# Row maxima computed one query block ahead of their scores, with a head's integer keys kept on chip

## The reference

```python
q = (x @ Wq + bq).reshape(1, B * N, H, hd)          # 1600 queries, H = 16 heads of hd = 16
kv = (cond @ Wkv + bkv).reshape(1, -1, 2, H, hd)    # 23104 keys
q = _fq_sym(q * scale, axis=-1)                     # 8 bit per row: step * integer
k = _fq_sym(k, axis=-1)
v = _fq_sym(v, axis=2)
attn = softmax(einsum('bhqd,bhkd->bhqk', q, k))
attn = _fq_unsigned(attn, axis=-1)                  # round(attn / (row maximum / 255))
out = einsum('bhqk,bhkd->bhqd', attn, v)
```

## Time and profile before

| | us |
|---|---|
| median of 3 runs | 8869.47 (8868.29 to 8872.59) |
| the profiled execution | 8867.96 |
| its span in the trace | 8866.1 |
| PE busy | 8189.6 (92%) |
| DVE busy | 6542.9 (74%) |
| ACT busy | 5480.9 (62%) |
| POOL busy | 5204.2 (59%) |

### The profile page before, as it was taken

One profiled execution on the slowest core, in us unless ns is written; L12 is line 12 of the kernel. 1 busy time (PEld: TensorE's weight loads), 2 busy tenths in 40 slices (PEclk: granted clock), 3 DMA queues, 4 the chain that ended last, 5 costly groups with the idle time before them and its releaser, 6 DMA issues.

```text
span 8866.1 us, 223739 instructions
## 1 busy us (share of the span) xinstructions
PE 8189.6 (92%) x60312; PEld 2600.3 (29%) x60312; DVE 6542.9 (74%) x6161; ACT 5480.9 (62%) x12138; POOL 5204.2 (59%) x3573
## 2 busy tenths in 40 slices
PE   8954999999999999999999999999999999988688
PEld 4510222222222222222222222222222222222343
DVE  8989777777777777777777777777777777720466
ACT  2300776767676767676767676767767676767333
POOL 5733665656565656565656565656656565666356
PEclk9955999999999999999999999999999999999789
DMA  5663011110102020202020202010111101020000
GB/s 162 209 163 93 12 26 20 21 24 18 27 13 33 11 34 12 34 12 34 12 34 12 34 11 34 12 28 17 25 20 24 21 18 28 17 42 7 10 4 4
DMA packets 305414, 303.94 MB, mean 34 GB/s; under 512 B 50718, under 2 KB 297802, under 8 KB 300458
## 3 DMA queue, kind: packets, MB, share of 16 engines
q1 hardware_dynamic: 304682, 303.13, 15.7%
q10 hardware_dynamic: 672, 0.16, 0.0%
HBM read 226.31 MB, written 76.71 MB: 34 GB/s over the span
## 4 chain that ended last, share of the span: by engine, by line
PE 63%; DVE 17%; issue 13%; POOL 2%; DVEq 1%; ACT 1%; DMA 1%; SPq 0%; ACTq 0%; POOLq 0%
PE psum L1395 21%; PE psum L1364 18%; DVE mpart L1185 14%; PE psum L1322 13%; PE psum L1374 4%; PE psum L1287 2%; POOL mix L391 1%; ACT y L1084 1%; PE psum L653 1%; DVEq L1185 1%; PE psum L1356 1%; DVE act_c L532 1%; PE psum L1420 1%; POOL kq L933 1%; POOL kq L926 1%
## 5 line engine op out<-in xcount | busy, mean ns | idle before, releaser
L1185 DVE TENSOR_REDUCE mpart<-psum 128x978 f32 x4992 | 5654.8, 1172 | 1510.3 <-PE psum L1322 1399.1
L1084 ACT ACTIVATE y<-psum 128x400 f32<-128x400 f32 x11520 | 5082.2, 504 | 2078.9 <-PE psum L1395 2011.6
L1004 POOL TENSOR_SCALAR xh<-y 128x1600 f16<-128x1600 f32 x2880 | 4397.9, 1527 | 2830.7 <-PE psum L1374 2025.1
L1395 PE MATMUL psum<-QT,K 99*128 x11520 | 3104.3, 340 | 61.0 <-ACT y L1084 54.7
L1364 PE MATMUL psum<-y,ones 128*17 128x400 f32 x23048 | 2539.2, 507 | 0.0
L1322 PE MATMUL psum<-K,QS 48*128 48x489 bf16 x9984 | 1782.8, 390 | 322.6 <-DVE mpart L1185 207.6
L1395 PEld LDWEIGHTS psum<-QT,K 99*128 x11520 | 879.3, 97 | 2495.0 <-issue 2294.7
L1374 PE MATMUL psum<-xh,vwin 128*16 128x400 f16 x11528 | 1019.6, 335 | 0.7 <-POOL xh L1004 0.7
L1322 PEld LDWEIGHTS psum<-K,QS 48*128 48x128 bf16 x9984 | 464.7, 93 | 1680.1 <-issue 873.5
L1364 PEld LDWEIGHTS psum<-y,ones 128*17 128x17 f32 x23048 | 402.4, 95 | 618.2 <-issue 617.8
L1374 PEld LDWEIGHTS psum<-xh,vwin 128*16 128x16 f16 x11528 | 322.6, 90 | 628.6 <-POOL xh L1004 364.5
(11 more groups left out here) (180 smaller groups left out, 2138.6 us busy)
## 6 DMA issues: line engine op xcount, KB each, us to landing
K<-kT_parts SPq DMA_DIRECT2D x204, 240.0 KB, 8.3
vwin<-v_int SPq DMA_DIRECT2D x579, 80.0 KB, 1.9
K<-kT_parts SPq DMA_DIRECT2D x772, 45.8 KB
kT_parts<-part SPq DMA_DIRECT2D x135, 256.0 KB, 3.2
K<-kT_parts SPq DMA_DIRECT2D x102, 242.0 KB, 8.4
src<-in_ctx_dram SPq DMA_DIRECT2D x46, 512.0 KB, 4.6
v_float<-kv SPq DMA_DIRECT2D x45, 512.0 KB, 5.2
vin<-v_float SPq DMA_DIRECT2D x9, 2560.0 KB, 10.1
```

What stands on the lines that cost most here:

```text
L1004: pool.tensor_scalar(xh[:, g % YR, :, :], y[:, g % YR, :, :], INT_STEP, 0.0, ALU.mult, ALU.add)\
L1084: act.activation(y[:, s % YR, j, :], s2_bank(GT * s + j), ACT.Exp).then_inc(exp_done, 1)
L1185: dve.tensor_reduce(mpart[:, t, ds(2 * cp + j, 1)], s1_buf(n)[:, :, 0:CHALF], AX.XY, ALU.max)\
L1395: pe.matmul(s2_bank(t), K3[0:MROW, h % 2, ds(c * REGION + t * P, P)], queries, start=True, stop=True).then_inc(s2_ready, 1)
```

## The change

Jobs of the maxima pass run one **block** ahead of their scores instead of one head. A block's 400 queries are three tiles of 128 (`PT` = 3) and 16 rows that are left; the 4 x 16 rows left of a head share one extra tile. A block's 3 bodies hold 3 x 24 jobs of the next block and 6 of the extra tile of the next head: 26 in a body, as before. Nine of the 72 ("lead") are for the block after the next, done after the turn of maxima. The prologue has 96 jobs and 9 lead jobs in place of 312. All 16 heads now hold jobs; those of the last block are for a head that does not exist and are not used.

`maxima` now comes once a block, inside body c = 2: DVE before the jobs of group 10, the transpose in group 12 between tiles 1 and jobs, ACT's copy between exp 1 and exp 2 of group 12, and three DMAs on SP (six at a head's end) in place of one on ACT. The first job after it uses the PSUM buffer that ACT's copy frees.

All 24 chunks of integer keys of a head stay in `K1`; they are exchanged for the next head's in block 2 of each head, in three bursts on SP (11, 8 and 5 chunks, two DMAs each, after bodies 0, 1 and within body 2, the last ahead of the maxima's rows in the queue). The extra tile has its own two chunks a body (`K1X`). `K3` is kept once; its region c is overwritten after body c of the last block. The three bodies of a block are written out, so that `K3`, `K1` and `QS` addresses are constants. In groups 1, 4, 7, 12 the second of two jobs goes behind tile 3. Values are stored and loaded in 4 KB rows, with two `vin` and `vo` buffers. The FFN weights load before the main loop instead of in the last head.

```diff
-CHUNKS = 2 * BODIES
+CHUNKS = 24
-JOBS = 2 * QT_TILES
-JOBS_AT = [2] * 10 + [1] * 4 + [2]
+PT = 3
+CB = CHUNKS // BODY_C
+LEADC = 3
+LEAD = PT * LEADC
+JOBS = PT * CB + 2
+OWN = JOBS - LEAD
+EXTRAS = (5, 11)
+JOBS_AT = [2, 2, 1, 2, 2, 1, 2, 2, 1, 2, 1, 2, 2, 2, 2]
+SPLIT = (1, 4, 7, 12)
+TURN_AT = 12
+PRO_SLOTS = 4 * CHUNKS + 2 + LEAD
+K1_PIECES = ((0, CB + LEADC), (CB + LEADC, 2 * CB + LEADC), (2 * CB + LEADC, CHUNKS))
+ROUND_AT = (5, 7, 8, 10, 12, 14, 16, 18, 20)
-EPI_SLOT = 13
+EPI_SLOT = 6
+def job_of(c, k):
+    if k < OWN:
+        if k in EXTRAS:
+            return PT, EXTRAS.index(k), False
+        i = k - sum(x < k for x in EXTRAS)
+        return i % PT, CB * c + LEADC + i // PT, False
+    i = k - OWN
+    return i % PT, (CB * (c + 1) + i // PT) % CHUNKS, c == BODY_C - 1
...
+            load_qs(QS, 0, 0, qs_in)
+            load_qs(QX, 0, BLOCKS * MAIN, qx_in)
+            for chunk in range(4):
+                load_k1(0, chunk)
             load_vin(0)
+            for chunk in range(4, K1_PIECES[0][1]):
+                load_k1(0, chunk)
+            load_qs(QL, 0, MAIN, ql_in)
+            load_vin(1)
+            for chunk in range(K1_PIECES[0][1], CHUNKS):
+                load_k1(0, chunk)
...
+            def block(h, b, last, turn=-1):
+                for c in range(BODY_C):
...
+                    for q in range(VPARTS):
+                        if q < 2:
+                            after_job(at + EXTRAS[q])
+                            load_k1x(head, 2 * nxt + q, q)
...
+                        if q == 1 and c == BODY_C - 1:
+                            after_job(at + OWN - 1)
+                            load_tiles(QS, h, b, 2, turn, qs_in)
+                            if turn == 2:
+                                for chunk in range(*K1_PIECES[2]):
+                                    load_k1((h + 1) % H, chunk)
+                        if q == 2:
+                            if c == BODY_C - 1:
+                                sp.wait_ge(mt_copied, block_of(h, b) + 2)
+                                load_m(m_in, (h + (1 if end else 0)) % 3, 0 if end else b + 1)
+                                if end:
+                                    load_m_tail((h + 1) % 3)
+                                after_job(at + JOBS + 1)
+                                load_tiles(QL, h, b, 3, turn, ql_in)
+                            if turn == 2 and c < 2:
+                                after_job(at + JOBS - 1 + (2 if c == 0 else 0))
+                                for chunk in range(*K1_PIECES[c]):
+                                    load_k1((h + 1) % H, chunk)
+                        sp.wait_ge(pv_done, YR + groups_before(h, b, c) + 5 * (q + 1))
+                        load_values(q, (h + ahead) * 9 + 3 * ((c + 1) % BODY_C) + q)
...
# scalar engine, in body
+                        if c == BODY_C - 1 and s == TURN_AT and j == 2:
+                            n = sum(JOBS_AT[:TURN_AT])
+                            mt_copy(block_of(h, b) + 1, h + 1, s1_at(h, b, c), n, job_buf(n))
...
# vector engine: prologue, then body
+            for chunk in range(CHUNKS):
+                for t in range(PT + 1):
+                    n = (PT + 1) * chunk + t
+                    job(t, slice(chunk, chunk + 1), 0, n, s1_buf(n))
+                if chunk in ROUND_AT:
+                    round_values(ROUND_AT.index(chunk))
             dve.wait_ge(vx_scaled, 1)
             dve.tensor_scalar(vox[:].rearrange("p h d -> p (h d)"), vinx[:], RNE, -RNE, ALU.add, ALU.add)\
                 .then_inc(vx_round, 1)
+            maxima(0, 0, 4 * CHUNKS)
...
+                    if c == BODY_C - 1 and s == 10:
+                        turn = block_of(h, b) + 1
+                        maxima(turn, turn % (BLOCKS * H), at + n)
...
# tensor engine: prologue, then body
+            for chunk in range(CHUNKS):
+                for piece, (first, end) in enumerate(K1_PIECES):
+                    if first == chunk:
+                        pe.wait_ge(k1_in[piece], 32 * (end - first))
...
+                if c == 0:
+                    pe.wait_ge(m_in, 48 * (B + 1))
...
-                        pe.matmul(s2_bank(t), K3[0:MROW, h % 2, ds(c * REGION + t * P, P)], queries,
+                        pe.matmul(s2_bank(t), K3[0:MROW, c * REGION + t * P:c * REGION + (t + 1) * P], queries,
                                   start=True, stop=True).then_inc(s2_ready, 1)
...
                     score_tile(s, 0)
                     score_tile(s, 1)
-                    next_jobs(JOBS_AT[s])
+                    if c == BODY_C - 1 and s == TURN_AT:
+                        maxima(B + 1, at, done, job_buf(done))
+                        extra = 2
+                    next_jobs(1 if s in SPLIT else JOBS_AT[s])
                     score_tile(s, 2)
                     score_tile(s, 3)
+                    if s in SPLIT:
+                        next_jobs(1)
```

More of the change, by code:

```diff
@@ L324, in s1_buf, with job_buf @@
             return psum[:, 2 * (n % 2):2 * (n % 2) + 2, :]
+        def job_buf(n):
+            return s1_buf(PRO_SLOTS + n)
         def s2_bank(j):
@@ L829, in load_ffn @@
+            for r in range(1, BODY_C):
+                load_region(0, r)
+            sp.wait_ge(q_in, 192)
+            load_q(1, 1)
             def load_ffn(part):
@@ L880, in _ @@
-            for piece in range(2):
-                sp.wait_ge(qs_in[piece], 96 * (H + 1))
+                with sp.Fori(0, 2) as b:
+                    block(h, b, False)
+                for b in range(2, BLOCKS):
+                    block(h, b, False, b)
+            with sp.Fori(0, 2) as b:
+                block(H - 1, b, True)
+            for b in range(2, BLOCKS):
+                block(H - 1, b, True, b)
+            for piece, (first, end) in enumerate(K1_PIECES):
+                sp.wait_ge(k1_in[piece], 32 * (end - first) * (H + 1))
@@ L1072, in body @@
                 for s in range(GROUPS):
-                    if not later and s == LAG_PV:
+                    if c == 0 and s == LAG_PV:
                         act.wait_ge(summed, YR + groups_before(h, b, 0))
@@ L1310, in _, with job @@
             last.then_inc(qi_turned, 1)
-            def job(head, cp, t, j, at, n, first=False):
-                if t == 0:
-                    pe.wait_ge(k1_in[j], 32 * (BODIES * head + cp + 1))
-                for piece in range(2):
-                    if first and j == 0 and t == QS_PARTS[piece][0]:
-                        pe.wait_ge(qs_in[piece], 96 * (head + 1))
+            def job(tile, keys, at, n, buf):
                 pe.wait_ge(s1_free, at + n + 1)
@@ L1321, in job, with tile_of, maxima @@
                     top, end = HALVES[k]
-                    last = pe.matmul(s1_buf(n)[:, k, 0:CHALF], QS[top:end, t * P:(t + 1) * P], K1[top:end, j, 0:CHALF],
-                                     start=True, stop=True)
+                    last = pe.matmul(buf[:, k, 0:CHALF], tile[top:end, :], keys[top:end, :], start=True, stop=True)
                 last.then_inc(s1_ready, 1)
-            def maxima(head, at):
-                pe.wait_ge(m3_ready, head + 1)
-                pe.wait_ge(s1_free, at + 2)
-                pe.transpose(psum[0:3 * QT_TILES, 0, :].bitcast(BF16)[:, 0:P], m3[:].rearrange("p a t -> p (a t)"),
+            def tile_of(t, lead):
+                if t == PT:
+                    return QX[:]
+                return (QL if lead else QS)[:, t * P:(t + 1) * P]
+            def maxima(turn, at, n, buf):
+                pe.wait_ge(m3_ready, turn + 1)
+                pe.wait_ge(s1_free, at + n + 2)
+                pe.transpose(buf[0:3 * (PT + 1), 0, :].bitcast(BF16)[:, 0:P], m3[:].rearrange("p a t -> p (a t)"),
                              identb[:]).then_inc(s1_ready, 2)
```

491 lines of the change are left out of this document (262 added, 229 removed).

## The result

The changed kernel takes **9109.16 us** (median of 4 runs, 9101.27 to 9120.13) against 8868.88 before: ratio 1.027, 95% interval 1.025 to 1.029. Forecast were 8479. The profiled execution took 9115.02 us, its span is 9112.8.

A forecast was written before the change was run, and what follows sets the result against it. PE's tile order, ACT's exp and DVE's reductions were taken to pace the heads, DVE the prologue. Prologue -161, 15 heads -252 and last head +22 gave -391, so 8479 us; range 8400 to 8660.

The forecast's parts named there:

- The rule set aside: Loop edges: a taken branch to a target outside a two-page window forces an instruction fetch; the forecast counted no cost.
- the fourth rival: Block loop's edge: PE stops at each of 64 edges until instructions return, 3.4 us each, +218 us, 8697; chance 3%.
- The turn of maxima: Body 2 of each block: DVE's seven operations, buffer wait, transpose and copy add 1.9 us, from +1 to +3.
- The prologue: Before the main loop: fewer jobs bring the first score at about 720, -161 us, bounds -180 and -140.
- The body: Body 1 of a block: address and split gains bring it from 37.0 to 35.5 us, -1.5.
- Constant addresses: One-job groups in the bodies: constant K3 addresses take them from 2.32 to 2.18 us; bounds nothing and 0.14.
- The splits: Groups 1, 4, 7, 12: second job behind tile 3 costs 2.47 us; unsplit pairs then take 2.39 to 2.45.
- Bursts of keys: Block 2 of each head: key loads delay the maxima's rows, 1.5 us a head; rival of 6 us late, 8551, 12%.
- The rival on the slower side: Every block: maxima's rows late because SP is behind; 7 us late gives 8927; chance 5%.

The follow-up runs named there:

- Two heads a pass: Changed kernel with POOL's rounding held back and PE's and ACT's programs written out for two heads per loop pass: 8530 us, against 8574 with one head.
- POOL's wait: POOL's group 10 rounding in body 2 waits for the split maxima: 8574 us with PE's and ACT's heads written out (8702 without), 8946 on the changed kernel.

## Why the prediction was wrong

The error is 630 us, and the chain of kernels divides it, in the order in which the edits were added: PE's edges inside a head 254, ACT's 153, POOL beside the turn 128, half of the heads' edges 45. That leaves 8530, 51 above the forecast. Two heads a pass took away 8 of 15 edges between heads; the other seven are about another 39 (estimate, 45 / 8 each), and the prologue was 14 late.

- **The rule set aside: the step that failed.** "By that rule every edge of both kernels should stall, and the longer block of the new one no less; by the rows it doesn't." The rows showed loops of some 1530 (PE) and 310 (ACT) instructions without a stall. They could not speak for one of 2104 and one of 463. I had counted neither, and gave the fourth rival 3%. Its price was 3.4 us an edge. PE's idle time was 4.2 on average, and PE's edge cost 4.7 us a block (121.1 to 116.4) with the tiles behind it at the 1.2 GHz level, and ACT's 3.9 more (116.4 to 112.5), which the rival did not have at all. The Trainium skill, page "Runtime: NRT & Kernel Launch", section "Instruction fetch mechanics", gives PE a store of 2048 instructions and most others 512. For PE the runs agree (some 1530 go round, 2104 and 2275 don't); for ACT 457 already stall, and its window of two pages of 256 does not fit PE's 1530. Where the limits lie between these numbers was not tried.
- **The turn of maxima.** "DVE's seven operations take about 1.5 us" was taken from a head's end and the prologue, where POOL did nothing. Beside POOL they took 3.1 us, and body 2 45.1 with the edge, 40.5 without it. With POOL held back, 37.8 was measured and 37.9 forecast: the rest of the step (buffer wait, transpose, copy) was sized right. The Trainium skill, page "SBUF — State Buffer", section "SBUF: two separate sides", says that a DVE operation in a two-port mode, or with two SBUF inputs against a GpSimd operation that reads SBUF, and a GpSimd operation lock each other out for a whole instruction, whichever starts first. The traces agree (1.36 us, ending with POOL's; in the prologue 13.57 us of DVE where POOL was first, 13.48 us of POOL where DVE was). Whether the one-input operations that waited ran in a two-port mode, no run here shows.
- **The prologue**: -161 forecast, -147 measured. What was late was the values, by 13 us at `vox`. The prediction had all nine roundings at 2.8 us; two of them waited for a whole multiplication of POOL, 10.75 us each. In the four runs in which only one did, `vox` came at 697.5 to 698.3 and the first score at 727 to 728. That the waits are the same lock follows from their starts and ends in the traces; no run kept the two apart.
- **The body**: right in its sum (35.5), wrong in its credit. Constant addresses with h left in a register gave one-job groups 2.26 (PE's bodies written out before), with h gone 2.18, as forecast. The splits bring 0.25 us in body 1; that the rest is where the one-job groups stand is argued, since no run moved them.
- **Bursts of keys**: right. With POOL's wait, block 2 is 1.4 us longer than block 1 (1.5 forecast), and the first tile behind it, block 3's, waits 1.39 us for the DMA of the rows.
- **The rival on the slower side** named rows late in every block. The rows were late only in block 2; the kernel became slower by mechanisms that stood elsewhere.

So the idea of the change was worth about what was forecast, and two side effects of its form took all of it and 240 us more.

## What to carry to other kernels

Before a loop body is written out, count the instructions of one pass for each engine, register instructions included, from the trace: here loops of some 1530 on PE and 310 on ACT were free, 2104 and 457 cost 2 to 5 us a block, and the cure was not a shorter body but fewer edges, since straight code of four and of eight blocks ran without a gap. A duration read where another engine was idle is a lower bound, and a mean can hide two lengths: when short DVE operations move beside POOL's, ask what they would wait for, and consider one semaphore wait to put them into POOL's gap.

## What the runs showed of the hardware

- DVE's operations on four columns in SBUF, with two tensor inputs or with one, cast or scalar, ended 3 to 28 ns after POOL's running operation when that one had started first; the DVE reductions, from SBUF (0.25 us) or PSUM (1.16), did not wait. The turn's second cast, which started 0.03 us ahead of POOL's operation, took its usual 0.17 us.
- The same held for long ones: a rounding of 2.8 us that started 0.07 us behind POOL's multiplication took 13.57 us (the fourth and the eighth of nine), and in the kernel with group 11 split a multiplication of 10.96 us that started 0.17 us behind a rounding took 13.48.
- Instruction packets of 16 KB on PE's queue arrive all through straight code, 8.8 in a block of some 2100 instructions, and leave no gap. With a jump back in each block there are 10.7, and PE idles 4.2 us on average at 2104 instructions a pass; inside the heads of the kernel before it idles 3.0 at 2275.
- PE's branch took 4.67 us (median) in the changed kernel, and 3.3 to 4.0 in the kernel before with PE's bodies written out and in those with heads written out. Why was not tried.
- The same stall on ACT left 2.2 to 2.3 us idle, of which three score banks covered 0.8 and 1.3.
- Two to three microseconds of idle PE were followed by stretches of 3.4 and 6.8 us at a granted clock of 0.50 (1.2 GHz), which added two thirds to what the stall cost in the kernel before with PE's bodies written out: 2.9 us at the edge, and 1.9 in the body behind it (half of the 3.4 us at that clock would be 1.7, an estimate).
